# Attention scores on the two row halves of TensorE: one group of heads per half, a third bank for the scores, reads of 4 KB a row

## The chip, the core and the metric

The kernel runs on one core of one Trainium2 chip. Five engines of the core work side by side and meet at semaphores: TensorE (matmuls, PE in the profile; its weight loads PEld), VectorE (DVE), ScalarE (ACT), GpSimd (POOL) and SyncE (SP), whose queue issues all DMAs here. The metric is the device time in microseconds, the median of several runs.

## What is computed

One gated cross-attention layer and one gated feed-forward layer over 8 sequences of 256 tokens with 512 features:

```python
x = x + tanh(g_xattn[0]) * attention(layernorm(x), ctx, ctx, Wq, Wk, Wv, Wfc, bfc)
x = x + tanh(g_ffn[0]) * ffn(layernorm(x), router, sh_gate, sh_up, sh_down, r_gate, r_up, r_down)

# attention: 32 heads of 16 features, 8 groups of keys and values, 4 heads per group
qh = (q @ Wq.T).reshape(N, S, 32, 16).transpose(0, 2, 1, 3)
kh = repeat((k @ Wk.T).reshape(N, S, 8, 16).transpose(0, 2, 1, 3), 4)   # vh likewise
score = einsum('bhqd,bhkd->bhqk', qh, kh) / sqrt(16)
out = einsum('bhqk,bhkd->bhqd', softmax(score), vh)
return out @ Wfc.T + bfc
# ffn: (g * sigmoid(g) * u) @ down.T, once with 2048 shared features, once with 256 routed
# ones that are weighted by the sum of the softmax over the two largest of 8 router logits
```

Everything is float32. The kernel reaches that accuracy with matmuls of the faster type f32r by splitting each operand into a high and a low part and adding three products (`three`, lines 1239 to 1243).

## The kernel before

The work has two stages. The attention stage covers four blocks of two sequences (512 tokens). The FFN stage follows, with fast matrix products in the manner of Strassen (`product`, `quad`, `down`), 18 blocks of 128 hidden features for each half of the tokens. The change does not touch the FFN's instructions.

The attention stage is a loop of 32 steps, 8 in each block (the first and last block written out, the two between them in a hardware loop, `blocks`). A step n covers one sequence and 8 heads, which are two groups of 4 heads that share keys. It does the following, in eight units u, on all engines at once.

- Scores for the maxima: `sm_unit` (line 1288) computes, two steps ahead, the scores of two heads and 128 queries against 256 keys, in two matmuls of 256 columns into one bank of PSUM, bank 0 or 1 in turn. VectorE takes the row maxima (`maximum`, line 881). A PSUM bank is used again when the maximum before last is done (the wait on `max_ok`).
- The 16 columns of maxima are turned by a matmul with the identity (`mt_job`, line 1320) into bank 5, ScalarE copies them, negated, into `mT` (`m_copy`), and SyncE writes them by DMA as one further row of `q_st` (`put_max`, line 297).
- Transposed scores: `st_unit` (line 1300) computes keys against queries with that row included, so that the maximum is already subtracted: one matmul of 512 columns into bank 2 or 3. ScalarE takes the exponential into `probs`; a bank is used again when its exponential is done (the wait on `exp_ok`).
- Values: `pv_unit` (line 1309) multiplies the probabilities with the values, on four column strips of the array at a time, into bank 4; a fourth of it per `p`, two visits of two in a step. VectorE turns bank 4 into `oB` (`o_turn`, line 989), divides by the sums and turns again into `aT`; ScalarE and VectorE split that into its high and low part.
- Fillers: between these, TensorE does the normalised input's transposes (`x_job`), the projections of the next block (`q_part`, `kv_part`) and the output projection of earlier work (`f_part`), three matmuls of 512 columns a part. They stand at fixed units of fixed steps, most of them in one half of a step.

The score operands have 48 rows: the high part of q, the high part again, and the low part (against high, low and high of k). Rows 48 to 63 of `q_st` are set to zero once, and `SM = P // 2 + 1` = 65 rows are used, 66 for the transposed scores:

```python
SM = P // 2 + 1
MROW = SM
ST = MROW + 1
```

The 48 rows come through memory: SyncE writes each projected chunk to `q_scr` and reads it back in another arrangement, in three DMAs per step with rows of 1 KB (`read_q`, line 277), when all transposed scores of the step before are issued. k takes the same way once a sequence.

Order is set by hand: every engine runs its list in order, and a wait at the head of TensorE's list holds everything behind it. In the last block, steps 1 to 4 also carry the FFN's first transposes (`x2_job`); GpSimd builds the FFN's inputs from them (`differences`, `split_x`) and then splits the first weights (`split_gu`).

## Time and profile before

| | us |
|---|---|
| median of 3 runs | 951.03 (944.7 to 956.66) |
| the profiled execution | 942.72 |
| its span | 940.9 |
| TensorE busy | 899.5 (96%) |
| VectorE busy | 646.6 (69%) |
| GpSimd busy | 486.7 (52%) |
| ScalarE busy | 343.4 (37%) |

A matmul's time in the profile runs to its modelled end, while the next one starts earlier; what a matmul costs in a row of them is the distance between starts. Idle time is named with what ended it.

### The profile page before, as it was taken

How to read it: one execution, taken by the hardware profiler on the slowest of the kernel's cores; microseconds unless marked ns; L12 is line 12 of the kernel's file. 1: busy time of each engine (PE TensorE's matmuls, PEld its weight loads, DVE VectorE, ACT ScalarE, POOL GpSimd, SP SyncE). 2: the span in 40 equal slices, each digit the busy share in tenths (PEclk: the TensorE clock that was granted, in tenths of full speed). 3: DMA queues.
4: the chain of work that ended last, by engine and by line, in shares of the span. 5: the costliest groups of instructions: out<-in, count | busy, mean ns of one | idle time of the engine just before them, and what ended most of it. 6: DMA issues, size and time to landing. Idle time of an engine off the chain costs nothing.

```text
span 940.9 us, 14873 instructions
## 1 busy us (share of the span) xinstructions
PE 899.5 (96%) x4896; PEld 697.8 (74%) x4896; DVE 646.6 (69%) x1083; ACT 343.4 (37%) x637; POOL 486.7 (52%) x485
## 2 busy tenths in 40 slices
PE   4689999999999999999999999999999999999998
PEld 3556766676677665688888888887688888888887
DVE  6678888778878887566656566567766656566566
ACT  5165566556655686212212122136212211122112
POOL 4201201300130299878766696663778766696650
PEclk9789999999999999999999999999999999999999
DMA  8863344435343420211111121111312111121102
GB/s 277 201 144 80 78 116 74 108 80 118 62 96 83 87 37 25 90 45 67 45 60 52 45 67 45 45 57 56 112 45 68 45 54 57 45 67 45 45 1 89
DMA packets 42346, 70.83 MB, mean 75 GB/s; under 512 B 5312, under 2 KB 21184, under 8 KB 42048
## 3 DMA queue, kind: packets, MB, share of 16 engines
q1 hardware_dynamic: 42304, 70.29, 27.9%
q8 instruction: 24, 0.39, 0.2%
q14 instruction: 18, 0.15, 0.1%
HBM read 55.33 MB, written 14.68 MB: 74 GB/s over the span
## 4 chain that ended last, share of the span: by engine, by line
PE 72%; issue 17%; DVE 4%; DMA 3%; POOL 2%; ACT 2%; SPq 0%; POOLq 0%; DVEq 0%; ACTq 0%
PE bank L1241 21%; PE bank L1243 20%; PE bank L1242 20%; PE bank L1316 3%; PE bank L1296 3%; PE bank L1306 3%; PE bank L1246 1%; POOL xa L461 1%; DMA q_scr<-qx_l 1%; POOL cx_l L430 1%; DVE mcol L887 1%; PE bank L1565 1%; DVE x_l L1206 1%; DMA wfc_raw<-wfc 1%; DMA xa<-x 1%
## 5 line engine op out<-in xcount | busy, mean ns | idle before, releaser
L887 DVE TENSOR_REDUCE mcol<-bank 128x2 f32<-128x512 f32 x256 | 169.8, 677 | 48.9 <-PE bank L1296 48.1
L1241 PE MATMUL bank<-x_l,w_h 128*128 128x512 f32 x504 | 197.5, 392 | 2.7 <-DVE u L1077 2.5
L1243 PE MATMUL bank<-x_h,w_h 128*128 128x512 f32 x504 | 196.4, 390 | 0.0
L1242 PE MATMUL bank<-x_h,w_l 128*128 128x512 f32 x504 | 196.4, 390 | 0.0
L740 ACT ACTIVATE probs<-bank 128x512 f32<-128x512 f32 x256 | 150.1, 594 | 120.6 <-PE bank L1306 119.5
L595 ACT ACTIVATE hT_h<-bank 128x512 fp32r<-128x512 f32 x72 | 43.2, 599 | 360.3 <-DVE bank L1179 351.5
L551 POOL TENSOR_TENSOR w_l<-raw,w_h 128x512 fp32r<-128x512 f32 (+1 forms) x144 | 162.1, 1159 | 2.9
L1089 DVE SCALAR_TENSOR_TENSOR xa<-bank,tgf,xa 128x512 f32<-128x512 f32 x128 | 96.1, 751 | 77.7 <-PE bank L1243 77.6
L1296 PE MATMUL bank<-k_st,q_st 65*128 65x256 f32 x512 | 114.0, 312 | 11.8 <-DMA q_st<-q_scr 7.1
L1296 PEld LDWEIGHTS bank<-k_st,q_st 65*128 65x128 f32 x512 | 92.9, 201 | 43.1 <-DVE mcol L887 16.6
L430 POOL TENSOR_TENSOR cx_l<-cx_raw,cx_h 128x512 fp32r<-128x512 f32 x12 | 15.5, 1295 | 191.4 <-ACT cx_h L595 191.4
L1241 PE MATMUL bank<-dn_l,hT_h 128*128 128x512 f32 x288 | 112.2, 390 | 1.6 <-issue 1.6
L1241 PEld LDWEIGHTS bank<-x_l,w_h 128*128 128x128 f32 x504 | 94.6, 188 | 25.7 <-DVE u L1077 3.7
L1243 PE MATMUL bank<-dn_h,hT_h 128*128 128x512 f32 x288 | 112.2, 389 | 0.0
L1242 PE MATMUL bank<-dn_h,hT_l 128*128 128x512 f32 x288 | 112.2, 389 | 0.0
L1243 PEld LDWEIGHTS bank<-x_h,w_h 128*128 128x128 f32 x504 | 94.6, 188 | 19.8
L1242 PEld LDWEIGHTS bank<-x_h,w_l 128*128 128x128 f32 x504 | 94.7, 188 | 19.3
L1306 PE MATMUL bank<-q_st,k_st 66*128 66x512 f32 x256 | 102.3, 403 | 2.3 <-ACT probs L740 1.8
L1077 DVE TENSOR_TENSOR u<-bank,r 128x512 f32<-128x512 f32 x72 | 49.8, 691 | 68.5 <-PE bank L1243 68.3
L560 POOL CAST dn_h<-dnraw 128x512 fp32r<-128x512 f32 x36 | 22.1, 613 | 111.9 <-PE bank L1243 92.5
L548 POOL CAST w_h<-raw 128x1792 fp32r<-128x1792 f32 x36 | 63.6, 1768 | 29.8 <-DVE x_l L1206 18.0
L1316 PE MATMUL bank<-probs,vals 128*32 128x256 f32 x1024 | 70.1, 392 | 0.0
(148 smaller groups left out, 1362.8 us busy)
## 6 DMA issues: line engine op xcount, KB each, us to landing
raw<-w_gu SPq DMA_DIRECT2D x36, 512.0 KB, 3.3
q_st<-q_scr SPq DMA_DIRECT2D x96, 128.0 KB, 3.8
dnraw<-w_dn SPq DMA_DIRECT2D x36, 256.0 KB, 2.6
xa<-x SPq DMA_DIRECT2D x4, 1024.0 KB, 7.6
cx_raw<-ctxT SPq DMA_DIRECT2D x16, 256.0 KB, 3.4
q_scr<-qx_h SPq DMA_DIRECT2D x16, 256.0 KB, 2.1
q_scr<-qx_l SPq DMA_DIRECT2D x16, 256.0 KB, 2.2
out<-xa SPq DMA_DIRECT2D x16, 256.0 KB, 2.0
```

The source lines that it names most:

```text
L548: g.tensor_copy(w_h[f][:, :, :], raw[f][:, 0:7, :]).then_inc(gu_hi, 1)
L551: last = g.tensor_tensor(w_l[f][:, part, :], raw[f][:, part, :], w_h[f][:, part, :].bitcast(f32), ALU.subtract)
L740: nc.scalar.activation(probs[:, p, 2 * (u % 2):2 * (u % 2) + 2, :], STB[u % 2][:, :].rearrange("p (r q) -> p r q", r=2), ACT.Exp, scale=fl ...
L887: v.tensor_reduce(mcol[:, par, at:at + 2], bank[u % sm_banks(n)][:, :].rearrange("p (r k) -> p r k", r=2), AX.X, ALU.max).then_inc(max_ok, 1)
L1077: return v.tensor_tensor(out, psum[:, :], part[:, :], ALU.add)
L1089: v.scalar_tensor_tensor(tile, source[:, :], scale, tile, ALU.mult, ALU.add).then_inc(acc_ok, 1)
L1241: mm(out, a_h, b_l, start=start, stop=False, skip_group_check=onto)
L1242: mm(out, a_l, b_h, start=False, stop=False, skip_group_check=onto)
L1243: return mm(out, a_h, b_h, start=False, stop=stop, skip_group_check=onto)
L1296: last = mm(bank[u % banks][:, j * S:(j + 1) * S], q_st[0:SM, c, h, qt * P:(qt + 1) * P], k_st[0:SM, bb, 2 * c + g2, :], start=True, stop= ...
L1306: mm(STB[u % 2][:, :], k_st[0:ST, bb, 2 * c + g2, kt * P:(kt + 1) * P], q_st[0:ST, c, h:h + 2, :], start=True, stop=True).then_inc(st_full, 1)
L1316: last = mm(OTB[32 * r:32 * r + VW, g2 * S:(g2 + 1) * S], vals[:, bb, kt, 2 * c + g2, :], probs[:, p, r, :], start=kt == 0, stop=kt == 1)
```

## The change

- Two heads of different key groups are computed side by side. The rows of one group lie in partitions 0 to 47 of `q_st` and `k_st`, those of the other in partitions 64 to 111, and the rows of maxima in partition 48 and 112. `sm_pair` issues four matmuls of 256 columns, `st_pair` two of 512, alternately on the lower and the upper rows, each half into a bank of its own. SM becomes 48 and ST 50. The zeroed rows and their memset go.
- The scores for the maxima have three banks, 0, 1 and 5. The transposed maxima move from bank 5 to bank 4, which is also the values' bank, with the waits this needs (`ob_ok` ahead of the transpose, `mt_cp` ahead of the values).
- A step is four quarters v. In each the transposed scores of the present step stand first, then the scores two steps ahead, then values, transposes and fillers. The fillers get new places, one or two parts in most quarters.
- The rows of Wq and Wk are permuted on the host, so that a read of q or k takes rows of 4 KB. A read of q is four DMAs instead of three and waits for the values of the step before last (`scored`). A chunk of q is written in 1 KB pieces.
- `aT` has two halves, and its splits have a place of their own for each sequence of a block; `w_h0` and `w_l0` move out of the memory that attention uses.

```diff
-CONSTS = 2
-SM = P // 2 + 1
+CONSTS = 1
+SM = 3 * DH
 MROW = SM
 ST = MROW + 1
+ROWS = P // 2
...
-        def sm_banks(n):
-
-            return 4 if isinstance(n, int) and n < 2 else 2
+        def sm_bank(n, s, u):
+
+            return bank[u % 4] if isinstance(n, int) and n < 2 else bank[(0, 1, 5)[(UNITS * s + u) % 3]]
...
+            def scored(n):
+
+                sp.wait_ge(pv_ok, 4 * n)
...
             def read_q(tb, bb, c, n, fresh):
+
                 if not fresh:
-                    sp.wait_ge(st_full, UNITS * n)
+                    scored(n)
                 sp.wait_ge(q_wr[c], 32 * (tb + 1))
-                for row, part in ((0, 0), (DH, 0), (2 * DH, 1)):
-                    src = q_scr[part, tb, c, :, bb * S:(bb + 1) * S].rearrange("(h d) q -> d h q", d=DH)
-                    sp.dma_start(r(q_st[row:row + DH, c, :, :]), src).then_inc(q_rd[c], 16)
+                for e in range(2):
+                    at, rows = e * ROWS, slice(e * ROWS, (e + 1) * ROWS)
+                    sp.dma_start(r(q_st[at:at + 2 * DH, c, :, :]).rearrange("p h q -> p (h q)"),
+                                 q_scr[0:2, tb, c, bb, rows, :].rearrange("a (d h) q -> a d (h q)", d=DH)).then_inc(q_rd[c], 16)
+                    sp.dma_start(r(q_st[at + 2 * DH:at + 3 * DH, c, :, :]).rearrange("d h q -> d (h q)"),
+                                 q_scr[0, tb, c, bb, rows, :].rearrange("(d h) q -> d (h q)", d=DH)).then_inc(q_rd[c], 16)
...
-            def sm_unit(n, u, bb, c):
-
-                qt, g2, half = u // 2 % 2, u // 4, u % 2
-                banks = sm_banks(n)
-                if not (isinstance(n, int) and n == 0 and u < banks):
-                    pe.wait_ge(max_ok, UNITS * n + u + 1 - banks)
+            def sm_pair(n, s, v, bb, c):
+
+                qt, half = v // 2, v % 2
+                if isinstance(n, int) and n < 2:
+                    if UNITS * n + 2 * v >= 4:
+                        pe.wait_ge(max_ok, UNITS * n + 2 * v - 2)
+                else:
+                    pe.wait_ge(max_ok, UNITS * n + 2 * v - (0 if s == 0 and v == 0 else 1))
                 for j in range(2):
-                    h = g2 * RH + half * 2 + j
-                    last = mm(bank[u % banks][:, j * S:(j + 1) * S], q_st[0:SM, c, h, qt * P:(qt + 1) * P],
-                              k_st[0:SM, bb, 2 * c + g2, :], start=True, stop=True)
-                last.then_inc(sm_full, 1)
+                    for e in range(2):
+                        rows = slice(e * ROWS, e * ROWS + SM)
+                        last = mm(sm_bank(n, s, 2 * v + e)[:, j * S:(j + 1) * S],
+                                  q_st[rows, c, 2 * half + j, qt * P:(qt + 1) * P], k_st[rows, bb, c, :],
+                                  start=True, stop=True)
+                        if j == 1:
+                            last.then_inc(sm_full[e], 1)
 
-            def st_unit(n, u, bb, c):
+            def st_pair(n, v, bb, c):
 
-                g2, kt, half = u // 4, u // 2 % 2, u % 2
-                if not (isinstance(n, int) and n == 0 and u < 2):
-                    pe.wait_ge(exp_ok, UNITS * n + u - 1)
-                h = g2 * RH + half * 2
-                mm(STB[u % 2][:, :], k_st[0:ST, bb, 2 * c + g2, kt * P:(kt + 1) * P], q_st[0:ST, c, h:h + 2, :],
-                   start=True, stop=True).then_inc(st_full, 1)
+                kt, half = v // 2, v % 2
+                if isinstance(n, int) and n == 0 and v == 0:
+                    pe.wait_ge(max_ok, 2 * UNITS)
+                else:
+                    pe.wait_ge(exp_ok, UNITS * n + 2 * v)
+                for e in range(2):
+                    rows = slice(e * ROWS, e * ROWS + ST)
+                    mm(STB[e][:, :], k_st[rows, bb, c, kt * P:(kt + 1) * P], q_st[rows, c, 2 * half:2 * half + 2, :],
+                       start=True, stop=True).then_inc(st_full[e], 1)
...
             def mt_job(n, par):
+
                 pe.wait_ge(max_ok, UNITS * n + UNITS)
-                tr(TPB[0:16, 0:P], mcol[:, par, :]).then_inc(mt_tr, 1)
+                if not (isinstance(n, int) and n < 2):
+                    pe.wait_ge(ob_ok, n - 1)
+                tr(OTB[0:16, 0:P], mcol[:, par, :]).then_inc(mt_tr, 1)
...
-                    for u in range(UNITS):
-                        if look:
-                            if u == 0:
-                                pe.wait_ge(q_rd[ce], 48 * (2 * te + be + 1))
-                                pe.wait_ge(k_rd[be], 48 * (te + 1))
-                            sm_unit(n + 2, u, be, ce)
-                        if u == 0:
+                    for v in range(UNITS // 2):
+                        if v == 0:
                             pe.wait_ge(m_rd, 32 * (n + 1))
-                        st_unit(n, u, bb, c)
+                        st_pair(n, v, bb, c)
+                        if look:
+                            if v == 0:
+                                pe.wait_ge(q_rd[ce], 64 * (2 * te + be + 1))
+                                pe.wait_ge(k_rd[be], 64 * (te + 1))
+                            sm_pair(n + 2, e % STEPS, v, be, ce)
```

TensorE's list before, the last two units of step 2 of a block in the hardware loop. Row L1296 are the scores for the maxima, L1306 the transposed scores, L1241 to L1243 one part of a projection; the names before the arrow are what is written, those behind it what is read.

```order
L1296 MATMUL bank0<-k_st,q_st 128x256 x2
L1306 MATMUL bank2<-q_st,k_st 128x512
L1241 MATMUL bank7<-xnT_l,wq_h 128x512
L1242 MATMUL bank7<-xnT_h,wq_l 128x512
L1243 MATMUL bank7<-xnT_h,wq_h 128x512
L1293 REGISTER_ALU
L1296 MATMUL bank1<-k_st,q_st 128x256 x2
L1306 MATMUL bank3<-q_st,k_st 128x512
```

The same engine's list now, the third quarter of step 7 of a block (L1304 transposed scores, L1289 scores for the maxima, L1314 values, L1229 to L1231 one part of a projection):

```order
L1304 MATMUL bank2<-q_st,k_st 128x512
L1304 MATMUL bank3<-q_st,k_st 128x512
L1289 MATMUL bank0<-k_st,q_st 128x256
L1289 MATMUL bank1<-k_st,q_st 128x256
L1289 MATMUL bank0<-k_st,q_st 128x256
L1289 MATMUL bank1<-k_st,q_st 128x256
L1314 MATMUL bank4<-probs,vals 32x256 x8
L1229 MATMUL bank6<-wfc_l,aT_h0 128x512
L1230 MATMUL bank6<-wfc_h,aT_l0 128x512
L1231 MATMUL bank6<-wfc_h,aT_h0 128x512
```

Where each unit had two score matmuls, one transposed one and then perhaps a part, six score matmuls now stand together, in two banks at a time, and between two such groups stands other work.

SyncE's list now, in steps 4 and 5 of a block in the hardware loop: a write of k, the maxima's row of the next step, a read of k, the write of the first chunk of q, and the read of that chunk.

```order
L314 DMA q_st<-mT 1x8x128 x2
L302 REGISTER_ALU
L305 DMA k_st<-k_scr 16x1024
L307 DMA k_st<-k_scr 32x1x1024
L305 ISA
L305 DMA k_st<-k_scr 16x1024
L307 DMA k_st<-k_scr 32x1x1024
L279 DMA q_scr<-qx_h 128x2x256
L279 ISA
L279 DMA q_scr<-qx_l 128x2x256
L268 REGISTER_ALU
L296 DMA q_st<-q_scr 32x1x1024
```

Before, the first chunk of q was written in step 3 (line 271 there) and read three issues at a time; its write now directly precedes its read.

## Rows read from the trace of the kernel before

**Rows 1.** The page's first line.
```profile
span 940.9 us, 14873 instructions
```

**Rows 2.** Stretches: us; busy us (instructions) of PE, PEld, DVE, ACT, POOL; clock; DMA.
```profile
149.00:235.00 86.00, 83.48 (x592) 59.35 (x596) 69.46 (x121) 50.30 (x100) 10.28 (x8) 0.98 0.41 89
...
380.00:941.00 561.00, 553.39 (x2486) 452.25 (x2484) 347.70 (x552) 124.94 (x215) 383.51 (x387) 1.00 0.17 55
```

**Rows 3.** VectorE's read of the output bank: all 32 by line, then the 26th.
```profile
L992 DVE STREAM_TRANSPOSE oB<-bank x32: 706/717/718, 63.4 to 379.7; 128x512 f32<-128x512 f32 x32
...
329.69 0.72 DVE L992 STREAM_TRANSPOSE oB<-bank 128x512 f32<-128x512 f32 x1 [0.44 <-PE bank L1316]
```

**Rows 4.** Two steps of the second block, columns as in the second group.
```profile
193.20:205.00 11.80, 11.80 (x82) 8.73 (x82) 8.54 (x15) 5.78 (x11) 0.00 (x0) 1.00 0.08 26
205.00:214.50 9.50, 9.28 (x70) 6.51 (x70) 7.72 (x14) 5.50 (x11) 0.00 (x0) 1.00 0.50 125
```

**Rows 5.** TensorE in order of time: start, us, line, what, count.
```profile
201.95 0.39 PE L1243 MATMUL bank<-xnT_h,wq_h 128*128 128x512 f32 x1
202.18 0.40 PE L1296 MATMUL bank<-k_st,q_st 65*128 65x256 f32 x2
202.41 0.40 PE L1306 MATMUL bank<-q_st,k_st 66*128 66x512 f32 x1
202.64 0.40 PE L1241 MATMUL bank<-xnT_l,wq_h 128*128 128x512 f32 x1
...
203.58 0.39 PE L1306 MATMUL bank<-q_st,k_st 66*128 66x512 f32 x1
203.90 1.07 PE L1316 MATMUL bank<-probs,vals 128*32 128x256 f32 x16
204.90 0.50 PE L1241 MATMUL bank<-xnT_l,wq_h 128*128 128x512 f32 x1
```

**Rows 6.** In order of time: latency to ScalarE, four transposes, behind the values.
```profile
151.21 0.40 PE L1306 MATMUL bank<-q_st,k_st 66*128 66x512 f32 x1
...
151.65 0.60 ACT L740 ACTIVATE probs<-bank 128x512 f32<-128x512 f32 x1
...
152.63 0.60 PE L1246 MATMUL bank<-ident,xn 128*128 128x128 f32 x4
152.99 0.36 PE L1296 MATMUL bank<-k_st,q_st 65*128 65x256 f32 x1
...
154.63 0.50 PE L1296 MATMUL bank<-k_st,q_st 65*128 65x256 f32 x2
154.97 0.40 PE L1306 MATMUL bank<-q_st,k_st 66*128 66x512 f32 x1
```

**Rows 7.** Waits from 63 to 320 us (total, times, longest); two maxima in time.
```profile
PEld bank L1296 <- DVE mcol L887: 13.1, 26, 0.8
...
PE bank L1296 <- DVE mcol L887: 4.5, 15, 0.5
...
306.78 1.28 DVE L887 TENSOR_REDUCE mcol<-bank 128x2 f32<-128x512 f32 x2
```

**Rows 8.** Chain of waits near the opening; SyncE's queue; DMAs, median us to landing.
```profile
57.08 4.24 DMA q_st<-mT
...
206.26 1.30 SPq L283 DMA_DIRECT2D q_st<-q_scr  x3
...
q_st<-q_scr SPq DMA_DIRECT2D x42, 128.0 KB, 3.8
q_scr<-qx_h SPq DMA_DIRECT2D x8, 256.0 KB, 2.1
```

**Rows 9.** GpSimd and TensorE at the end of attention, in order of time.
```profile
329.36 0.72 POOL L499 TENSOR_TENSOR xs<-xs 128x256 f32<-128x256 f32 x1 [15.57 <-ACT xs L595]
...
370.57 4.70 POOL L551 TENSOR_TENSOR w_l<-raw,w_h 128x512 fp32r<-128x512 f32 x4
...
379.58 0.50 PE L1241 MATMUL bank<-x_l,w_h 128*128 128x512 f32 x1
```

More of the change, by code:

```diff
@@ L338, in body @@
                     n = STEPS * t + s
-                    if s + 3 < STEPS or not last and s != 6:
+                    if s + 3 < STEPS or not last:
                         e = s + 3
@@ new lines, in body @@
+                        if not first:
+                            if s in (1, 2) and u == 3:
+                                f_sum(t - 1, 1, s - 1)
+                            if s == 1 and u == 7:
+                                f_stats(t - 1, 0, 1)
+                            if s == 2 and u == 6:
+                                f_stats(t - 1, 1, 0)
+                            if s == 3 and u == 4:
+                                f_stats(t - 1, 1, 1)
+                        if last:
+                            if (s, u) in ((5, 3), (6, 1)):
+                                f_sum(t, 0, s - 5)
+                            if (s, u) in ((6, 4), (7, 4)):
+                                f_stats(t, 0, s - 6)
+                            if s == 0 and u == 0:
+                                dve.wait_ge(ln2_stats, HTILES)
+                                for i in range(HTILES):
+                                    aggregate(1, i, ln2_var)
+                            if s == 0 and u == 5:
+                                norm2_rows(0, 0, HTILES)
+                            continue
@@ L1356, in _ @@
             vt_job(0, 0)
-            pe.wait_ge(q_rd[1], 48)
-            for u in range(UNITS):
-                sm_unit(1, u, 0, 1)
+            pe.wait_ge(q_rd[1], 64)
+            for v in range(UNITS // 2):
+                sm_pair(1, 1, v, 0, 1)
             q_job(3, q_lo, 2)
@@ L1415, in body @@
-                        if s == 1 and u in (4, 6) and not last:
+                        if not first:
+                            if s == 0 and v == 0:
+                                pe.wait_ge(vt_cp, 2 * t + 1)
+                                f_part(t - 1, 1, 0, 0)
+                            if s == 0 and v in (1, 2):
+                                f_part(t - 1, 1, 0, v)
+                            if s == 1 and v == 0:
+                                f_part(t - 1, 1, 0, 3)
+                            if s == 1 and v == 2:
+                                pe.wait_ge(f_add, TILES * t - 1)
+                                f_part(t - 1, 1, 1, 0)
+                                f_part(t - 1, 1, 1, 1)
+                            if s == 1 and v == 3:
+                                f_part(t - 1, 1, 1, 2)
+                            if s == 2 and v == 1:
+                                f_part(t - 1, 1, 1, 3)
@@ L1441, in body @@
-                        if s == 5 and u < 4 and not last:
-                            if u == 0:
-                                pe.wait_ge(v_cp, nx + 1)
-                            f_part(t, 0, 1, part)
-                        if last and 2 <= s < 6 and u in (3, 6):
-                            if s == 2:
-                                if u == 3:
-                                    pe.wait_ge(vt_cp, 2 * t + 2)
-                                else:
-                                    pe.wait_ge(f_add, TILES * t)
-                            f_part(t, 0, u // 6, s - 2)
@@ L1476, in body @@
-                        if s == 7 and u == 5 and not last:
-                            pe.wait_ge(q_lo, CHUNKS * nx + 3)
+                                pe.wait_ge(f_add, TILES * t - 2)
+                            x_job(nx, 0)
+                        if s == 0 and v == 3:
+                            pe.wait_ge(x_lo, TILES * nx + 1)
+                            x_job(nx, 1)
+                        if s == 1 and v in (1, 3):
+                            pe.wait_ge(x_lo, TILES * nx + 2 + v // 2)
+                            x_job(nx, 2 + v // 2)
@@ new lines, in body @@
+                        if s == 2 and v == 0:
+                            pe.wait_ge(x_lo, TILES * nx + 4)
+                            vt_job(t, 1)
+                        if s == 2 and v == 1:
+                            pe.wait_ge(vt_cp, 2 * t + 2)
+                            kv_part(nx, 0, 0)
+                        if s == 2 and v == 2:
+                            if not first:
+                                pe.wait_ge(f_add, TILES * t)
+                            kv_part(nx, 1, 0)
```

501 lines of the change are left out of this document (245 added, 256 removed).

## Prediction

> **What bounds the kernel now.** I read the stretches by stage first, then single instructions of TensorE, then the waits. [rows 1] give the profiled span, 940.9 us, of a run that took 942.7; the median of the three runs shown is 951.0, 8.3 above it. [rows 2] cut the span into stages. From 380 us on comes the FFN, 561 us in which TensorE is busy 553; the change leaves its instructions alone. What it changes lies between about 46 and 380 us. There, as 149 to 235 us shows, TensorE is busy 97% of the time and VectorE 81%, so TensorE's order of work sets the pace, with VectorE not far behind.
>
> A step is one pass of the loop over 8 heads. [rows 3] mark steps by the transposed read of the output bank, which comes once a step: the first at 63.4 us, the 26th at 329.69, so 25 steps of 10.65 us. [rows 4] show two: one of 11.8 us that TensorE fills, and one of 9.5 that it nearly fills, with VectorE at 8.5 and 7.7; by [rows 2] VectorE's mean is 0.81 x 10.65 = 8.6.
>
> **TensorE's own time in a step.** Single instructions are in [rows 5]. Start to start, a 512-column matmul of a projection takes 0.23 us (201.95 to 202.18), two score matmuls of 256 columns 0.24 (202.18 to 202.41), one transposed score matmul of 512 columns 0.23 (202.41 to 202.64). The probabilities-times-values group of 16, which uses column strips, takes 1.00 (203.90 to 204.90), its start comes 0.32 after the score matmul ahead of it instead of 0.23, and the first matmuls behind it hold the engine 0.34 instead of 0.24 ([rows 6], 154.63 to 154.97). So a visit costs 0.09 + 1.00 + 0.10, 1.20. I read the 0.09 as the array emptying before its division changes, and the 0.10 as a weight load that could not be made ahead. The 1.00 must hold a second emptying of about 0.1. Four 128-column transposes take 0.36 ([rows 6]).
> Per step: 15 projection matmuls 3.50; eight units of scores (0.24 + 0.23) 3.76; two visits 2.40; transposes 5 x 0.36 / 8 = 0.23. Sum 9.89. In the first block the 24 matmuls of a previous block's output projection are missing, 5.6 us or 0.22 a step over 25. The trace has 10.65, so 0.98 a step, 24 us in all, is waiting. [rows 7] name most of it: loads and matmuls of the scores wait 13.1 + 4.5 us for VectorE's maxima. That falls in units that have no projection work: such a unit is 0.47 us of TensorE against 0.64 of VectorE for one maximum (two in 1.28, [rows 7]). Before, the projections stand in one half of a step; the other half waits.
>
> **The change part by part.**
> Scores in row halves. The same 16 + 8 matmuls are issued, but in pairs whose halves use partitions 0 to 63 and 64 to 127. No row of this trace has two row halves at work. Bounds: no overlap, 3.76 a step; full, 1.88. The nearest row is the column-strip group: its 16 matmuls of 256 columns fit in 1.00 ([rows 5]), while 16 at the scores' 0.12 each would take 1.9. So parts of the array do work side by side. I take full overlap: -1.88.
> Changes of division. Score matmuls used 65 and 66 rows, and stood in the same division as the projections; 48 and 50 rows do not. A step now has four score groups. Going in costs 0.1 + 0.1, coming out the same: 0.40 for the two groups followed by projections, and 0.20 for the two that run into the values group, which had to be entered and left before too. +1.20 a step (bounds: 0.6 if only the emptying counts, 1.9 if weights stay bare inside the group, see below).
> Own time after: 9.89 - 1.88 + 1.20 = 9.21, less 0.22 for the first block: 8.99.
> Waiting. The projections are now cut into one or two parts in nearly every quarter of a step, so the maxima (two per quarter, 1.28, with the rest of VectorE's work 8.6 a step) run beside TensorE work of 2.3 us per quarter. A third bank gives no more lookahead in units than before (all but the last one or two maxima must be done), but no quarter is left without cover. I keep 0.6 of the 0.98 us: 9.59 a step. Bounds: 0.98 kept, 9.97; 0.2 kept, 9.19. Over 25 steps that is -26.5 us (-17 to -36).
> The transposed scores stand first: TensorE now waits at the group's head for both exponentials of the previous quarter. A first exponential starts 0.44 after its matmul ([rows 6], 151.21 to 151.65), two take 1.1 to 1.2, so the pair is done 1.7 us into a quarter of 2.3: hidden. A quarter with two extra jobs on ScalarE slips by the 0.6 it lacked, and the next absorbs it.
> Maxima into the output bank. Their transpose now waits for VectorE's read of the previous output. The read follows two maxima; the transpose stands one score group after the next quarter starts. About 0.6 us of room; nothing charged.
> SyncE. Reads of q become four issues instead of three (0.43 each, [rows 8]) and wait for the previous step's values groups. The maxima's row, two issues, stands behind them; it landed in 4.24 us in the one place where the chain shows it. Mostly it has a quarter to spare. Not so in one step per block: the write of the first q chunk is issued only at the end of step 4, the read in step 5 waits for its landing (2.1), then issues (4 x 0.43) and lands (3.8), and the maxima's row leaves behind it. I charge 0.5 us three times. The larger packets may shorten reads; I count nothing, since the full step of [rows 4] has DMA busy for 0.08 of it, so reads have room. The dropped GpSimd memset stands beside the first loads; nothing.
> Opening up to 63.4 us: ruled by loads, and by writes and reads of q, all of which stay. 0, bounds -2 to +2.
> End of attention. [rows 9]: GpSimd works without a gap from 329.36 to 370.57 + 4.70 = 375.3, on the FFN's inputs and last on the first weights, and TensorE starts the FFN at 379.58. The chain starts from a copy in step 2 of the last block, before and after the change, and stays as long. So of the last six steps no more than 379.6 - 375.3 = 4.3 us can be gained; GpSimd is late next. I take 3.5.
> **Sum**: -26.5 - 3.5 + 1.5 = -28.5. 942.7 becomes 914, the median **922 us**, own range 912 to 932.
>
> **The rivals.**
> A, the pair is not free: inside a group each weight load stays bare, and two 256-column matmuls take 0.34 instead of 0.24 as behind a values group in [rows 6]. With two such in a group that is +0.20 a group, +0.8 a step, +22 us: 944. For it: the loads of two halves may share one path. Against: the strips' loads do not hold their group.
> A2, the overlap is partial: between the bounds 1.88 and 3.76 a step's scores take 2.44, if a third of the second matmul sticks out of each pair. +0.56 a step, +16 us: 938. For it: the strips have to share the array too, and their 1.00 says nothing about how near that is to ideal. Against: 1.00 is already under what one after the other would take. The Trainium skill, "TensorE: Matmul & The Clock Gate", Part 3: Packing small matmuls, gives 3.07 times for four row tiles, 77% of ideal; as an estimate by that page two halves gain 1.54 times, which is this rival. No run here shows it yet.
> B, waiting moves: the maxima's transpose, the both-exponentials wait and the late row of maxima stop TensorE 1.4 us a step. Then 10.4 a step, -6 us: 945. For it: the engines meet once per quarter, and VectorE has 8.6 of 9.6 us to do. Against: the even spread, and 8.6 under TensorE's own 9.0. The Trainium skill, "TensorEngine Tiling (Array Packing)", PSUM Bottleneck, says that emptying PSUM may become the bound once tiling speeds TensorE up, which is this rival's side.
> C, slower: row halves run one after the other. Place: the score groups. Price: 3.76 stays and 1.20 is added, 0.38 of waiting goes: +0.82 in 25 steps, about +1 in the last six, +1.5: 979. It decides if the second of a pair starts after 80% of the first's time; at under half the change loses nothing. Against: the strips.
> D, better: nearly all waiting goes, 9.2 a step: 911 or less.
> A lower clock could join any of these: [rows 2] show a granted clock of 0.98 from 149 to 235 us, where TensorE idled 2.5 us, and pauses for emptying are idle time too.
>
> **How the numbers follow.** Forecast 0.50; D 0.13; A 0.10; A2 0.07; B 0.10; C 0.06; something slower still on the clock's side 0.04. The range 906 to 952 leaves about 0.07 below and 0.13 above. Measurement tells about 2%, 19 us: faster than 932 is forecast, D and a little of A2, 0.66; within 2%, the rest of A, A2 and B, 0.24; slower 0.10.
>
> **What would show it.** In the new trace: two transposed score matmuls starting within some 10 ns and a group of six in 0.5 us (else A, A2 or C); 0.3 to 0.4 from the last of a group to the next projection; steps of 9.4 to 9.8; fewer waits for maxima; GpSimd gapless up to the FFN's start, then an FFN of 561. It is wrong if steps stay over 10 us, or the FFN moves.

## The result, and the profile after

The changed kernel takes **1036.4 us** (median of 4 runs, 1030.5 to 1038.5), the kernel before on the same chip 953.9 (944.7 to 958.8): a ratio of 1.087, 95% interval 1.077 to 1.097. It is slower by 8.7%, where 922 us was forecast, and lies outside the range of 906 to 952. Its profiled run took 1036.4 with a span of 1034.5.

I cut the span at the same places as before: the first read of the output bank, the 26th, the last. The stretches of the changed kernel, with columns as in [rows 2], and its reads of the output bank, which answer to [rows 3]:

```profile
0.00:86.60 86.60, 42.43 (x196) 30.12 (x198) 42.49 (x76) 26.67 (x44) 11.04 (x17) 0.73 0.48 162
86.60:415.30 328.70, 260.95 (x1848) 155.32 (x1850) 207.69 (x390) 150.31 (x309) 36.25 (x32) 0.86 0.22 71
415.30:473.40 58.10, 46.55 (x373) 25.97 (x370) 38.19 (x68) 34.51 (x70) 47.11 (x50) 0.91 0.12 40
473.40:1034.50 561.10, 553.60 (x2486) 452.38 (x2486) 347.45 (x552) 124.92 (x215) 384.72 (x387) 1.00 0.17 55
```
```profile
L979 DVE STREAM_TRANSPOSE oB<-bank x32: 702/716/718, 86.6 to 473.4; 128x512 f32<-128x512 f32 x32
```

Before, the same four stretches were 63.4, 266.3, 49.9 and 561.3 us. So the opening lost 23.2 us, the 25 steps 62.4 (13.15 us each instead of 10.65), the last six 8.2, the FFN nothing. In the 25 steps TensorE is idle for 67.7 us, where it was idle for 7.7 of 266.3 before, and its granted clock is 0.86, where it was 0.98.

**TensorE's part went nearly as forecast.** A quarter of a step in the changed kernel, as [rows 5] (start, us, line, what, count):

```profile
160.09 0.50 PE L1304 MATMUL bank<-q_st,k_st 49*128 49x512 f32 x2
160.43 0.40 PE L1289 MATMUL bank<-k_st,q_st 48*128 48x256 f32 x4
160.76 0.28 PE L1234 MATMUL bank<-ident,mcol 128*16 128x128 f32 x1
160.79 0.48 PE L1229 MATMUL bank<-wfc_l,aT_h 128*128 128x512 f32 x1
161.10 0.40 PE L1230 MATMUL bank<-wfc_h,aT_l 128*128 128x512 f32 x1
...
162.02 0.39 PE L1231 MATMUL bank<-wfc_h,aT_h 128*128 128x512 f32 x1
162.34 0.50 PE L1304 MATMUL bank<-q_st,k_st 49*128 49x512 f32 x2
```

The two transposed scores start 3 ns apart by the trace's records (3 or 4 in all 128 pairs). The next instruction comes 0.34 after the pair and 0.33 after the four scores for the maxima, the first projection behind the group holds 0.31, and the last one ahead of the next group 0.32, where 0.23 is the usual distance. From group to group there are 2.25 us. (The transposed scores use 49 rows, where the prediction said 50 and the list of changes has "ST 50": the row of maxima is the 49th.)

**What went wrong shows in the waits.** Total, times and longest of those from 86 to 416 us. No score matmul waits for VectorE's maxima any more, as they did in [rows 7]; another wait stands in their place:

```profile
PEld bank L1304 <- DMA q_st<-mT: 70.9, 20, 9.9
...
PE bank L1304 <- DMA q_st<-mT: 65.1, 20, 9.5
```

TensorE waits for the row of maxima. (PEld are the weight loads, PE the matmuls behind them; these are almost the same waits seen twice, not two sums to be added.) The chain of waits across one step (start, us, what) tells where that row is:

```profile
206.84 0.70 SPq L296
...
207.64 0.35 SPq L298
...
208.17 0.69 SPq L296
...
208.97 0.35 SPq L298
...
210.63 0.70 SPq L314
...
211.38 6.33 DMA q_st<-mT
...
217.75 0.54 PE bank L1304 x2
```
```profile
214.54 0.39 PE L1231 MATMUL bank<-cx_h,wkv_h 128*128 128x512 f32 x1
217.75 0.54 PE L1304 MATMUL bank<-q_st,k_st 49*128 49x512 f32 x2 [2.83 <-DMA q_st<-mT]
```

SyncE issues the four reads of q, the loads of context, then the row, which leaves at 211.38 and lands 6.33 us later; TensorE had run dry 2.83 us before it could go on. Worked out from the landing records (last landing of a pair of issues, less its start), the row takes 6.4 us in the median of its 32 times, against 2.5 in the kernel before. Had it kept its 2.5 us it would have been there at 213.9, before TensorE needed it.

Why it takes so long shows in what the DMA engines move. The next step's transfers, from 222 to 232 us, in 40 slices of 0.25 us: first the busy share of the 16 engines in tenths, then GB/s.

```profile
DMA  0313803116222011201111110000000000000100
GB/s 0 33 33 82 213 33 115 66 49 246 66 49 78 33 66 45 49 33 49 49 49 49 49 66 35 35 16 21 0 0 0 0 0 0 0 0 0 33 0 0
```

The reads of a step come to 384 KB. They begin with a burst or two, but from 226 to 228 us the mean is 49 GB/s at a busy share of 0.13. The packets themselves (start in us, ns, bytes; "..." marks what is left out) say what that is:

```
225.187 28 512      226.810 160 4096     228.087 159 4096     228.599 159 4096
225.192 34 512      226.890 159 4096     228.133 159 4096     228.760 159 4096
225.219 28 512      226.967 162 4096     228.248  27  512     228.921  27  512
... (6 in all)      227.046 159 4096     228.277  27  512     228.950  27  512
```

Packets of 4096 bytes run in exactly two chains (226.810, 226.967, ... and 226.890, 227.046, ...), each beginning when the one before it in its chain has ended: 2 x 4096 bytes in 0.16 us are 51 GB/s. The maxima's row is two transfers of eight packets of 512 bytes. Six of the first are moved by 225.25, six of the second by 225.96. The last four come in two pairs, at 228.25 and 228.28 when the first chain is through, at 228.92 and 228.95 when the second is: each chain holds back one packet of either transfer. So two of the 16 DMA engines still have rows of q to fetch, and the row of maxima stands behind these rows on just those two. A two-part read has 32 rows of 4 KB; two engines share them, and there are two such reads in a step: 32 rows x 0.16 = 5.1 us for each of the two engines. The other two reads have 16 rows and are spread.

The difference between them is the order of their dimensions: the two-part read walks part (2), then head dimension (16), then 4 KB. The Trainium skill, "DMA: Bandwidth & Descriptors", Why a DMA increments its semaphore by 16 and not by 1, has the rule: a transfer gets the largest number of engines, up to 16, that divides the slowest dimension (of size over 1) of both its sides. For a slowest dimension of 2 that is two engines, and by the same page, for transfers such as SyncE issues, they are the lowest-numbered ones, which a row that goes to eight engines uses as well. The packet records name no engine, but they agree with both, with two chains and two late packets of eight.

Everything else that goes to 16 engines has a share on these two, and is late with it. Before, the loads of context took 3.4 us in the median, the writes of q's low part 2.2 and of k's 3.2. The changed kernel (KB each, median us to landing):

```profile
cx_raw<-ctxT SPq DMA_DIRECT2D x16, 256.0 KB, 7.1
q_scr<-qx_h SPq DMA_DIRECT2D x16, 256.0 KB, 2.8
q_scr<-qx_l SPq DMA_DIRECT2D x16, 256.0 KB, 4.3
...
k_scr<-kx_l SPq DMA_DIRECT2D x4, 256.0 KB, 6.5
```

In the one step of each block in which a write must land before a read is issued, both delays add up; that step takes 19 to 20 us in each of the three blocks that have it (the chain of waits, second block):

```profile
244.96 6.82 DMA q_scr<-qx_l
...
251.91 0.67 SPq L296
...
253.23 0.65 SPq L296
...
254.45 0.70 SPq L314
...
255.21 5.69 DMA q_st<-mT
```

The opening is the same chain: writes of 7.72 and 9.72 us, the load of the output projection's weights with 9.87 instead of 6.18, the first row of maxima with 7.29 instead of 4.24.

The granted clock adds to the loss. Three stretches behind one another:

```profile
138.30:149.80 11.50, 7.70 (x53) 4.65 (x51) 6.38 (x13) 4.22 (x9) 0.00 (x0) 1.00 0.27 82
149.90:160.00 10.10, 4.50 (x25) 2.25 (x25) 2.01 (x3) 1.57 (x3) 0.00 (x0) 0.50 0.21 76
160.10:170.00 9.90, 9.86 (x78) 6.03 (x79) 8.24 (x15) 4.79 (x10) 0.00 (x0) 1.00 0.28 95
```

TensorE idled 3.8 of the 11.5 us ahead of the stretch at 0.50 (the lower level, 1.2 GHz), and was gapless once it stood at 1.00 again. What it cost is worked out below, against a version without the idling.

### The profile page after: what moved, and what is told of

It reads as the page before. It is cut to its first block, busy times and chain, and to the rows that moved or that the text cites. A ratio compares the mean times of both kernels' runs of the same rounds, so it can differ in the third digit from the quotient of the medians.

```text
span 1034.5 us, 14797 instructions
## 1 busy us (share of the span) xinstructions
PE 903.5 (87%) x4896; PEld 663.8 (64%) x4896; DVE 635.8 (61%) x1083; ACT 336.4 (33%) x637; POOL 479.1 (46%) x484
## 4 chain that ended last, share of the span: by engine, by line
PE 65%; DMA 20%; SPq 8%; DVE 3%; issue 2%; ACT 1%; ACTq 0%; DVEq 0%
PE bank L1229 19%; PE bank L1231 18%; PE bank L1230 18%; DMA q_st<-mT 13%; PE bank L1314 4%; DMA q_scr<-qx_l 4%; SPq L296 3%; PE bank L1304 3%; DMA k_scr<-kx_l 2%; SPq L298 2%; SPq L314 1%; PE bank L1289 1%; DMA wfc_raw<-wfc 1%; PE bank L1234 1%; PE bank L1611 1%
## 5 line engine op out<-in xcount | busy, mean ns | idle before, releaser
L874 DVE TENSOR_REDUCE mcol<-bank 128x2 f32<-128x512 f32 x256 | 166.1, 676 | 147.9 <-PE bank L1289 146.7
L731 ACT ACTIVATE probs<-bank 128x512 f32<-128x512 f32 x256 | 138.7, 594 | 189.9 <-PE bank L1304 189.6
L1229 PE MATMUL bank<-x_l,w_h 128*128 128x512 f32 x504 | 197.3, 391 | 2.7 <-DVE u L1065 2.5
L1231 PE MATMUL bank<-x_h,w_h 128*128 128x512 f32 x504 | 196.2, 389 | 0.0
L1304 PE MATMUL bank<-q_st,k_st 49*128 49x512 f32 x256 | 73.0, 567 | 88.0 <-DMA q_st<-mT 83.6
L1304 PEld LDWEIGHTS bank<-q_st,k_st 49*128 49x128 f32 x256 | 27.0, 208 | 138.3 <-DMA q_st<-mT 91.1
L1229 PE MATMUL bank<-dn_l,hT_h 128*128 128x512 f32 x288 | 112.1, 389 | 1.7 <-issue 1.7
L1231 PE MATMUL bank<-dn_h,hT_h 128*128 128x512 f32 x288 | 112.0, 389 | 0.0
L1229 PEld LDWEIGHTS bank<-x_l,w_h 128*128 128x128 f32 x504 | 94.6, 188 | 25.8 <-DVE u L1065 3.7
L1231 PEld LDWEIGHTS bank<-x_h,w_h 128*128 128x128 f32 x504 | 94.6, 188 | 19.6
L1314 PE MATMUL bank<-probs,vals 128*32 128x256 f32 x1024 | 82.9, 450 | 0.0
L1289 PE MATMUL bank<-k_st,q_st 48*128 48x256 f32 x512 | 61.0, 323 | 17.5 <-DMA q_st<-q_scr 13.1
L1289 PEld LDWEIGHTS bank<-k_st,q_st 48*128 48x128 f32 x512 | 57.2, 227 | 27.0 <-issue 14.0
```

Source lines behind the costliest of these rows:

```text
L731: nc.scalar.activation(probs[:, p, 2 * half:2 * half + 2, :], STB[e][:, :].rearrange("p (r q) -> p r q", r=2), ACT.Exp, scale=float(DH) ** ...
L874: v.tensor_reduce(at[:, :, qt], sm_bank(n, s, u)[:, :].rearrange("p (r k) -> p r k", r=2), AX.X, ALU.max).then_inc(max_ok, 1)
L1229: mm(out, a_h, b_l, start=start, stop=False, skip_group_check=onto)
L1231: return mm(out, a_h, b_h, start=False, stop=stop, skip_group_check=onto)
L1289: last = mm(sm_bank(n, s, 2 * v + e)[:, j * S:(j + 1) * S], q_st[rows, c, 2 * half + j, qt * P:(qt + 1) * P], k_st[rows, bb, c, :], start= ...
L1304: mm(STB[e][:, :], k_st[rows, bb, c, kt * P:(kt + 1) * P], q_st[rows, c, 2 * half:2 * half + 2, :], start=True, stop=True).then_inc(st_ful ...
```

## Experiments

Theory 1: reads whose slowest dimension is 2 go to two DMA engines, and the row of maxima and the writes queue behind them. Theory 2: SyncE issues the row too late (reads held until the values groups, four issues ahead of the row). Theory 3: that the transposed scores stand first makes the whole group wait. Theory 4: long rows are slow in themselves. The kernel before ran beside each group of experiments and took 952.1 to 952.7 us there.

**Sixteen engines (e1_sixteen).** The dimensions of the two-part reads are turned; q's parts stand in the scratch in the opposite order, so that q interleaves (low, high) and k (high, low), and the three products stay the same. (For k the two-part read now also stands ahead of the one-part read.)

```
- q_scr[0:2, tb, c, bb, rows, :].rearrange("a (d h) q -> a d (h q)", d=DH)
+ q_scr[0:2, tb, c, bb, rows, :].rearrange("a (d h) q -> d a (h q)", d=DH)
```

> The changed kernel with one thing turned: the reads that fetch two parts of q (or k) at once walk head dimension first and part second, so that the slowest dimension of their source has 16 entries instead of 2; the rows of high and low parts stand interleaved in q_st and k_st, bytes, row length (4 KB), issues and order of issue are the same. Theory 1 (a read whose slowest dimension is 2 is carried by two DMA engines, 32 rows of 0.16 us for each of them per step, 5.1 us, and the row of maxima queues behind them): the row of maxima lands in 2.5 to 3.5 us instead of 6.4, TensorE's wait for it between the first and the 26th step falls from 65 us to under 10, the first step starts before 70 us instead of 86.6, and the time is 940 to 960. Theory 2 (SyncE holds the reads until the values groups and has four issues to make ahead of the maxima): these issues stay, so 1020 or more. Theory 3 (transposed scores first makes the whole group wait): 1020 or more, too. A fourth, that long rows are slow in themselves: 1020 or more.

**919.1 us** (918.7 to 920.4), ratio to the kernel before 0.965 (0.959 to 0.971), faster than the 940 to 960 that I expected. The row of maxima lands in 2.6 us. Its stretches, cut at the same reads (63.0, 304.3, 354.2), and its waits of the whole span:

```profile
0.00:63.00 63.00, 37.39 (x198) 26.82 (x199) 42.26 (x75) 26.59 (x44) 10.74 (x17) 0.85 0.61 209
63.00:304.30 241.30, 230.93 (x1848) 139.74 (x1846) 207.68 (x391) 150.11 (x309) 36.68 (x32) 0.99 0.31 100
304.30:354.20 49.90, 44.35 (x373) 24.88 (x369) 38.93 (x68) 34.38 (x70) 47.19 (x49) 0.97 0.15 47
354.20:916.80 562.60, 555.22 (x2486) 453.03 (x2486) 348.09 (x552) 124.96 (x215) 385.30 (x388) 1.00 0.17 55
```
```profile
PEld bank L1304 <- DMA q_st<-mT: 8.2, 9, 2.0
PE bank L1304 <- DMA q_st<-mT: 3.6, 4, 1.8
```

And one step's transfers in 40 slices of 0.25 us, from 186 us on:

```profile
DMA  0002999997000000027941065970000100799599
GB/s 0 17 0 82 340 344 348 340 365 271 8 0 0 0 0 0 0 66 229 328 131 33 0 115 147 393 181 0 6 10 0 25 8 0 258 348 332 164 336 344
```

The 340 GB/s from 187.0 to 188.5 are the writes of q. Its reads are issued from 189.03 on and come in two bursts, 48 packets of 4096 bytes from 190.49 to 191.45 us and 47 from 191.92 to 192.85; the row of maxima, issued from 191.87 on, is moved at 193.24, right behind them. In the changed kernel the same 96 packets took from 222.29 to 228.92. Bytes, rows and the number of issues are those of the changed kernel; one permutation of dimensions takes 117 us off. Theories 2, 3 and 4 as the main cause fall here. This version also gives the price of the clock: the same 1848 matmuls of the 25 steps kept TensorE busy 230.9 us at 0.99 and 261.0 at 0.86. So of the 117.7 us between the two spans, 57.4 are idle time in the 25 steps, 30.0 more busy time at the lower clock there, 23.6 the opening, 8.2 the last six steps, and -1.5 the FFN.

**Six reads (e11b_six_reads).** Another way to 16 engines: each two-part read is cut into two reads of one part.

```
- one read of q_scr[0:2, ...] into 2 * DH rows
+ for part in range(2): one read of q_scr[part, ...] into DH rows
```

> The changed kernel with each read of two parts cut into two reads of one part (16 rows of 4 KB each), so that every read's slowest dimension is 16: six issues instead of four per step, and nothing else moved. Theory 1 (number of DMA engines): the two-engine queue is gone here too; the row of maxima lands in under 3.5 us, and the time is near e1_sixteen: 918 to 928, with 0.7 us more of SyncE ahead of the row. Theory 2 (SyncE's issues ahead of the row): two issues more make it worse than the changed kernel, over 1036.

922.9 us (920.4 to 926.6), ratio 0.971 (0.966 to 0.976); the row lands in 2.5 us. More issues on SyncE, and still 114 us faster than the changed kernel. TensorE's matmuls wait 6.3 us for the row between 62 and 306 us (1.8 in e1_sixteen between 63 and 304), so theory 2 has a small true part: 3 to 4 us for two issues more in a step.

**A queue of its own (e2_own_queue).** The changed kernel, the row of maxima issued by ScalarE.

```
- sp.wait_ge(mt_cp, n + 1);  sp.dma_start(q_st[row of maxima], mT)      # SyncE
+ act.wait_ge(mt_cp, n + 1); nc.scalar.dma_start(q_st[row of maxima], mT)  # ScalarE, behind its copy
```

> The changed kernel, reads untouched (two parts at once), but the row of maxima is issued by ScalarE right behind its copy, on ScalarE's own DMA queue. Theory 1 with a strict queue (the row stands behind the reads in SyncE's queue): it lands in 2.5 to 3.5 us, steps fall from 13.15 to 10.5 to 11, the opening, whose writes and reads of q stay in SyncE's queue, keeps its 20 us, the time is 960 to 985. Theory 1 with the two engines themselves as the bottleneck for every queue: landing 4 us or more, time 990 to 1036. Theory 2 (issue time ahead of the row on SyncE): same gain as the strict queue, so this run does not part these two; the run with 16 engines does.

1011.0 us (1009.7 to 1013.7), ratio 1.061 (1.054 to 1.068). The row still takes 5.8 us in the median, so it is the two engines that are full, whatever queue feeds them, and theory 1 with a strict queue falls. The Trainium skill, "DMA: Bandwidth & Descriptors", Issuing engines are not separate DMA queues, says that the queues of different issuers run on the same 16 engines, and this run agrees. The 25 us gained are then the earlier issue, which no run shows by itself. The wait has spread over the reads as well (waits from 83.9 to 393 us):

```profile
PE bank L1284 <- DMA q_st<-q_scr: 36.0, 10, 9.6
...
PE bank L1299 <- DMA q_st<-mT: 16.3, 19, 2.4
```

**Two engines in the kernel before (e3_before_two), and long rows alone (e4_before_long).** Both write q with its rows ordered (d h) and read rows of 8 KB. The first fetches two parts in one read, the second keeps three reads of one part.

```
+ e3: q_scr[0:2, tb, c, bb, :, :].rearrange("a (d h) q -> a d (h q)", d=DH)     # slowest dimension 2
+ e4: q_scr[part, tb, c, bb, :, :].rearrange("(d h) q -> d (h q)", d=DH)        # slowest dimension 16
```

> The kernel before with one part of the change done alone: q is written with rows (d h), so that a read has rows of 8 KB, and the second high part and the low part are fetched by one read whose slowest dimension is 2 (two issues instead of three). Scores, groups, maxima and the release of the reads are as before. Theory 1: that read has 16 rows of 8 KB, about 0.32 us each, for each of two DMA engines, 5.1 us; the row of maxima lands in 5 to 7 us instead of 2.5, steps grow by 1 to 3 us, time 975 to 1035. Theories 2 and 3: one issue fewer, nothing else changed, 940 to 955.

> The kernel before with the rows of 8 KB but three reads of one part each, whose slowest dimension is 16, as many as before. Theory 1: the two engines are the cause and not the length, so no change, 940 to 960. If long rows are slow in themselves: the maxima land later than 4 us and the time is over 975.

e3: 1002.5 us (997.6 to 1004.8), ratio 1.053 (1.047 to 1.060); e4: 951.3 us (946.1 to 955.5), ratio 0.999 (0.996 to 1.002). Long rows cost nothing that these runs can tell; two engines cost 50 us in a kernel that has nothing of the change but them and the long rows. The row of maxima takes 5.2 us there, as expected, but TensorE's wait turned out to be for the reads of q themselves (waits from 81 to 384 us), which I had not said:

```profile
PE bank L1299 <- DMA q_st<-q_scr: 20.2, 6, 3.8
...
PE bank L1309 <- DMA q_st<-mT: 0.5, 2, 0.2
```

**The order in the group (e12b_order_in_changed, e5b_order_undone).** Scores for the maxima first again, once in the changed kernel and once in e1_sixteen.

```
- wait(m_rd); st_pair(n, v, bb, c)
  sm_pair(n + 2, e % STEPS, v, be, ce)
+ wait(m_rd); st_pair(n, v, bb, c)
```

> The changed kernel as it is, with only the order in the group turned back (maxima's scores first); reads still go to two DMA engines. Theory 3 (that the transposed scores stand first is what loses the time): under 970. Theory 1: the row of maxima still lands in 6.4 us, 2.6 too late in every step; only the pair of scores and the weights ahead of it are done meanwhile, 0.3 us a step, 8 to 10 us in all, and the wait moves behind them: 1022 to 1032.

> The version with 16 engines (e1_sixteen), with the order within each group of scores turned back: the pair of scores for the maxima of step n+2 first, the transposed pair of the present step second. If standing first costs something (the whole group waits for the row of maxima and for both exponentials), this is 5 to 10 us faster than e1_sixteen's 919: e1_sixteen shows 6 + 2 us of waits for the row and 3 + 2 us for exponentials in its 25 steps. If the order is neutral: 915 to 923. If it helps (the transposed scores start the exponentials earlier, which the last steps wait for), 3 to 10 us slower.

In the changed kernel 1021.3 us (1020.6 to 1028.0), ratio 1.075 (1.069 to 1.081): 15 us where 8 to 10 were expected, so theory 3 is not the main cause; TensorE's matmuls now wait 49.9 us for reads of q and 7.1 for the row. In e1_sixteen **914.3 us** (913.8 to 916.5), ratio 0.960 (0.957 to 0.964): the order costs 4.8 us once the reads are right. Between 62 and 306 us the weight loads of the transposed scores wait 9.2 us for the row and the exponentials when they stand first, 2.8 when they stand second.

**The release of the reads (e6b_early_reads), the row on ScalarE (e7b_own_queue).** Both on e1_sixteen; the edit of the second is that of e2_own_queue, of the first

```
- scored(n)      # sp.wait_ge(pv_ok, 4 * n)
+ for e in range(2): sp.wait_ge(st_full[e], UNITS // 2 * n)
```

> e1_sixteen with the reads of q released as in the kernel before, by the transposed scores of the step before, and not by its groups of values. Theory 2 in its weak form (the row of maxima stands behind late reads): the few late rows in e1_sixteen, 8 us of waits, go: 911 to 916. If the lateness is the landing itself, or those steps have other bounds: within 3 us of 919.

> e1_sixteen with the row of maxima issued by ScalarE behind its copy. Its issue no longer waits for SyncE's four reads, but costs ScalarE two issues of 0.69 us in a step (ScalarE is busy 150 of 241 us in the 25 steps). The 8 us of waits for the row go, and exponentials behind the issues come up to 1.4 us later: 911 to 916 if ScalarE has room for them, over 922 if the exponentials are then late (waits of TensorE for ScalarE over 10 us).

The early reads give 917.7 us (915.9 to 919.0), 1.4 less than e1_sixteen, which the spread of the runs nearly covers. ScalarE's queue gives 926.0 (922.5 to 929.4), 7 more: the waits for the row fall to 1.2 us, but those for exponentials rise from 2.2 + 3.1 to 6.1 + 12.5. So the weak form of theory 2 is worth at most 1 or 2 us, and on ScalarE the issues make the exponentials late.

**The halves on the same rows (e8b_one_row_group).** e1_sixteen with every score matmul on partitions 0 to 63, so that the heads of the upper half are computed from the lower half's rows.

```
- rows = slice(e * ROWS, e * ROWS + ST)
+ rows = slice(0, ST)
```

> e1_sixteen with every score matmul on partitions 0 to 63, so that no two of them can run side by side; instructions, sizes, banks and waits are the same (the heads of the upper half are computed from the lower half's rows, so this output is not the reference's). It measures the term of the prediction that counts most, -1.88 us a step for full overlap: own time grows by 1.88 a step, 32 steps, of which 31 lie on the path: 919 + 58 = 977, a bit less where VectorE's maxima or waits already filled the step (970). If the halves overlapped only in part, less: 940 to 955. It also tells what the change would have been without overlap (rival C).

972.8 us (963.1 to 976.6), ratio 1.019 (1.013 to 1.026), 53.8 more than e1_sixteen. A group there:

```profile
202.78 0.73 PE L1304 MATMUL bank<-q_st,k_st 49*128 49x512 f32 x2
203.35 0.63 PE L1289 MATMUL bank<-k_st,q_st 48*128 48x256 f32 x4
203.91 0.42 PE L1314 MATMUL bank<-probs,vals 128*32 128x256 f32 x4
```

The pair takes 0.57 where it took 0.34 and the four 0.56 where they took 0.33, 0.46 a group and 1.84 a step. Its 25 steps take 286.3 us (69.5 to 355.8), 45.0 more than e1_sixteen's. That would be 1.80 a step, but it is not all overlap, as the granted clock shows: the first two steps of this version, then the other 23, and the same 23 of e1_sixteen:

```profile
69.50:100.40 30.90, 30.90 (x137) 19.74 (x137) 16.37 (x30) 13.53 (x27) 2.86 (x4) 0.53 0.15 53
100.40:355.80 255.40, 254.26 (x1709) 167.51 (x1710) 190.98 (x360) 138.49 (x283) 33.22 (x29) 1.00 0.26 85
```
```profile
82.10:304.30 222.20, 213.11 (x1708) 129.55 (x1708) 190.86 (x361) 136.44 (x282) 32.80 (x29) 1.00 0.31 98
```

At the same clock TensorE is busy 1.79 us a step longer, and the step is 1.44 longer, since e1_sixteen idles 0.35 more of each. The first two steps lose 11.8 us against e1_sixteen's (19.1 us at 0.85) and the opening 6.5, mostly beside a lower clock (0.77 against 0.85 in the opening).

**Two banks (e10b_two_banks), and both edits (e9b_both).** The first is e1_sixteen with bank[u % 2] for the maxima's scores and the wait that goes with two banks, the second e1_sixteen with the order turned back and the early reads.

> e1_sixteen with two banks for the maxima's scores instead of three, as the kernel before had: a pair of them then waits for both maxima of the pair before, not for all but the last. The prediction said that the third bank adds no lookahead that counts. A quarter is 2.3 us long and holds two maxima, 1.28 us, that start 0.44 after their matmuls, so VectorE has 0.5 us to spare: 919 to 922 by that. If VectorE's other work (a read of 0.7, splits of 1.2 us) often stands between the two maxima, TensorE waits for them in a third of the quarters: 925 to 935.

> The version with 16 engines with both edits that helped by themselves: maxima's scores ahead of the transposed ones, and reads of q released by the transposed scores. The first took 4.8 us off, the second 1.4. With the order turned back the row of maxima is needed one pair (0.3 us) later and TensorE's waits for it are already down to 2 us, so the second edit has little left: 912.5 to 915, faster than the kernel before by 4%.

Two banks: 923.3 us (921.3 to 924.5), 4.2 more than three; this lies between the two cases, with waits of weight loads for maxima up from 1.0 to 5.5 us between 62 and 306. In the profiled runs 1.7 us of it lie in the 25 steps and 2.7 in the last six, where the granted clock was 0.94 instead of 0.97. Both edits: 914.7 us (911.7 to 916.6), ratio 0.961 (0.957 to 0.965), the same as the order alone. The best of all is the order turned back with 16 engines: 914.3, 4% below the kernel before, and 12% below the changed one.

## Why the prediction was wrong

- **SyncE, the step that failed.** I counted the issues of the reads and their release, took the row's landing as what [rows 8] show, and of the larger packets said that they may shorten the reads. I never asked how a two-part read is spread over the DMA engines. In place of the 1.5 us of the SyncE term the shape of these reads cost 117 (the changed kernel against e1_sixteen): the row of maxima landed in 6.4 us instead of 2.5. That the reads "have room" because the full step has DMA busy for 0.08 of it was the wrong inference: a low mean over 16 engines says nothing of two of them. The changed kernel's own 25 steps have a DMA share of 0.22, against 0.31 in e1_sixteen, for the same transfers in a longer time. By the prediction's own sign, steps over 10 us, it is wrong: they take 13.15.
- **TensorE's sum** was right in its total. Forecast 9.59 us a step; e1_sixteen, which has all of the change but the spread, takes 241.3 / 25 = 9.65. Full overlap: -1.88 a step taken, 1.84 from the starts and 1.79 from the busy time at the same clock. The group of six takes 0.67 instead of 0.5, because the sign left out the group's edges, which the sum had: by the starts each change of division costs 0.08 to 0.11 (0.32 ahead of the group, 0.34 for the pair, 0.33 for the four, 0.31 behind), 0.37 for a group between projections where 0.40 was taken.
- **Waits**: the split of the step is not confirmed. The prediction found 0.98 us a step of waiting before, added the weight loads' 13.1 and the matmuls' 4.5 (13 of those 15 waits of matmuls lie inside one of a weight load), and kept 0.6. Counted as idle time of TensorE, the kernel before has 7.7 us in the 25 steps, 0.31 each, and e1_sixteen 10.4, 0.42 each. So idle time did not fall; busy time did, by 1.11 a step (258.6 to 230.9), where the own time was to fall by 0.68. That the two misses cancel in 9.59 is luck.
- **Both exponentials and the row at the group's head, "hidden":** not quite. The order costs 4.8 us.
- **The third bank, no lookahead that counts:** two banks take 4.2 us more, 1.7 of it in the 25 steps.
- **The late release of the reads and the late row, 0.5 three times:** 1.4 us by e6b_early_reads, right in size, but barely measured.
- **Opening, 0 with bounds of 2:** -0.4 in e1_sixteen; +23.2 in the changed kernel, since writes, reads and the row of maxima all have a share on the two engines.
- **End of attention, -3.5:** this came out as 0; e1_sixteen has 49.9 us there, as before. GpSimd and TensorE in order of time, as [rows 9]:

```profile
305.08 0.74 POOL L493 TENSOR_TENSOR xs<-xs 128x256 f32<-128x256 f32 x1 [14.31 <-ACT xs L590]
...
346.46 4.66 POOL L546 TENSOR_TENSOR w_l<-raw,w_h 128x512 fp32r<-128x512 f32 x4
...
354.11 0.50 PE L1229 MATMUL bank<-x_l,w_h 128*128 128x512 f32 x1
```

  GpSimd's chain is as long as before, 46.0 us, and the slack behind it shrank from 4.3 to 3.0; but it starts 0.8 us behind the 26th read of the output bank instead of 0.3 ahead of it, which takes back 1.1. Why TensorE needs these 3.0 us wasn't tried.
- **The FFN:** 561.1 against 561.3, as forecast.
- **The rivals.** B named the right place, the late row of maxima, at 1.4 us a step with two other waits; the changed kernel idles 2.7 a step. C gave 979 for halves that run one after the other; e8b_one_row_group, which does that, has 972.8, but part of this is the lower clock of its first steps, so the nearness is in part luck. A, A2 and C did not occur. A third of a matmul sticking out would make A2's scores 2.5 us a step, not 2.44. The clock did fall, behind stretches in which TensorE waited; it stood at 0.99 in e1_sixteen's 25 steps. With the spread put right the time is 919, three off the forecast, and that is no credit to it: the change as given has the slow reads. It is also partly luck: from profile to profile e1_sixteen gains 24.1 us (940.9 to 916.8) where 28.5 were forecast, and the 8.3 us that the median before stood above its profiled run do not come back, since e1_sixteen's median is 0.4 above its own.

## What to carry to other kernels

When transfers are merged, look at the slowest dimension of both sides: a leading dimension of 2 puts the whole transfer on two DMA engines, and what is issued behind it, from another engine's queue too, waits for its share on them. Small, late transfers on which TensorE waits are hit first; in a trace this shows as a rate that stays near 50 GB/s with a busy share of about 0.13, and as landing times that grow for transfers that were not touched. A mean DMA share that falls may mean slower transfers, not fewer.

## What the runs showed of the hardware

- Two matmuls on partitions 0 to 63 and 64 to 127 with separate banks overlap in full: starts 3 ns apart, 0.34 us for a pair and the edge of its group against 0.57 on the same rows.
- A change between such a group and matmuls on all rows costs 0.08 to 0.11 us at each edge, seen in the distances between starts (0.31 to 0.34 instead of 0.23).
- Two DMA engines move rows of 4 KB at 49 GB/s, one packet in 0.16 us each; with 16 engines 48 such packets were through in 0.96 us.
- Row length alone did nothing to the time: rows of 8 KB instead of pieces of 1 KB, on 16 engines, 951.3 against 952.7 us.
- Of the eight packets of one small transfer six were moved at once and two 3.0 and 3.7 us later, since only two engines were full.
- The same 1848 matmuls cost TensorE 30 us more at a mean granted clock of 0.86 than at 0.99, and the fall shown came behind a stretch in which it idled. But e8b_one_row_group stayed at 0.50 from 60 to 95 us although TensorE had no gap there (busy 5.00 in each 5.00 us), so work without gaps did not bring the clock back at once. Its row-half matmuls ran one after the other; whether that matters was not tried.
